# Experts of a slot mixture on one Trainium2 core: dense inner values, up products transposed in four row tiles, two batches, the first one's outputs inside the loop

## The chip, the core and the metric

One core of a Trainium2 chip runs the kernel. Its engines work side by side, each through its own list of instructions: TensorE (PE) multiplies matrices into PSUM, VectorE (DVE), ScalarE (ACT) and GpSimd (POOL) do elementwise work and reductions, SyncE (SP) issues the transfers. Semaphores order them. The metric is the device time of one execution in microseconds; less is better.

## The reference

A small vision tower: 32 images of 36 patches, 1152 tokens of width 192, in float32. The change lies in the last part, the mixture of 8 experts with 4 slots each:

```python
Xn = l2_normalize(X, axis=-1)
sp = l2_normalize(slot_params, axis=1) * scale
logits = jnp.einsum('bmd,dnp->bmnp', Xn, sp)
D = jax.nn.softmax(logits, axis=1)
C = jax.nn.softmax(logits.reshape(b, m, n * p), axis=2).reshape(b, m, n, p)
X_tilde = jnp.einsum('bmd,bmnp->bnpd', Xn, D)
H = gelu(jnp.einsum('bnpd,ndh->bnph', X_tilde, W_down) + b_down[None, :, None, :])
Y_tilde = jnp.einsum('bnph,nhd->bnpd', H, W_up) + b_up[None, :, None, :]
Y = jnp.einsum('bnpd,bmnp->bmd', Y_tilde, C)
```

Ahead of it stand a patch embedding with two layer norms and a channel attention with a residual and a norm; behind it come another residual and the last norm. Each expert has 24 inner values.

## The kernel before

The tokens are worked on in 11 groups of three images (108 tokens; the last has two images, 72). Every step of the computation is a function of a group `g`, and the order on each engine is written out by hand: a loop over `s` calls the functions with staggered groups (`at(slot_in, s - 6)` works on group s - 6), in 17 steps on TensorE and ACT and 16 on DVE and POOL. Nothing is reordered by a scheduler; an engine that waits holds everything behind it.

For a group, the end of the loop is this chain. `turn_xn` (PE, L507) transposes the unit tokens xn, `take_xn` (ACT) copies them, `logits` (PE, L519) multiplies with the slots. `mask_logits` gives lm on DVE, from which come two softmaxes: mC, eC (over slots) and, by way of `turn_l` (L526), mD, eD (over tokens). DVE inverts the sums (rC, rD) and scales eD, `turn_dc` (L535, L536) transposes both, DVE takes dm and ACT takes cT, `slot_in` (L542) forms the slots' inputs, and `take_slots` copies them to xt (ACT, L1018). A table load on ACT stands wherever exponentials and gelus alternate.

The experts are worked in three batches of groups, `HB = ((0, 4), (4, 8), (8, NG))`. `hidden(b)` (L554) multiplies xt with the down weights: expert n lands in column tile n % 4, on 24 of its 32 partitions, and e = n // 4 is the half of the free axis. `gelu(b)` (L1026) writes `hb[128, 2, B, 8, 4]` one expert at a time into an array that was cleared before, so that each column (slot of expert n) is zero except on its own expert's 24 partitions. By this the up product of a group is two full products with all of hb as weights: `slot_out(g)` (L565), out of 96 slots by 192. The bias is added on DVE (`slot_bias`, yt, L855), `combine(g)` (L578) multiplies with cT, and DVE's `last_residual` (z, L862), `last_stats` (L870) and `last_moments` (L875), POOL's `ln4_root` (L1139, L1142), DVE's `last_shift` (L880) and ACT's `last_norm` (o, L1035) finish the group; SP sends it out.

hidden(0) and hidden(1) stand in TensorE's steps 13 and 14, gelu(0) in ACT's step 15, behind the last exponentials. All outputs come after the loop, eleven rounds of slot_out and combine. POOL clears wu and hb at the start.

## Time and profile before

| what | us |
|---|---|
| median of 3 runs | 141.26 (140.8 to 141.6) |
| profiled execution | 140.0 |
| its span, first to last instruction | 138.0 |
| PE busy in the span | 115.0 |
| DVE busy | 88.9 |
| ACT busy | 69.0 |
| POOL busy | 67.0 |

The busy times are sums over stages with different limits; PE's is not a measure of how near it is to its peak, since its matmuls are pipelined. The stages must be read one at a time: weights and inputs to about 33 us, the loop to about 117, the outputs from there.

### The profile page before, as it was taken

What the parts mean: (1) busy time and instruction counts of PE and PEld (TensorE: products, weight loads), DVE (VectorE), ACT (ScalarE), POOL (GpSimd) and SP (SyncE); (2) the same over time, 40 slices, a digit from 0 to 9 for tenths busy, and PEclk for the clock granted to TensorE, in tenths of its full rate; (3) what the DMA queues carried; (4) which work ended last, traced back from release to release, by engine and by line L of the source; (5) the groups of instructions that cost most, each with busy time, mean ns of one, the idle gap of its engine ahead of it and who ended that gap; (6) DMA issues with size and microseconds to landing.
All of it is one profiled execution on the core that took longest, in us unless ns stands there. A gap on an engine that the chain in (4) does not pass through costs nothing.

```text
span 138.0 us, 4819 instructions
## 1 busy us (share of the span) xinstructions
PE 115.0 (83%) x1779; PEld 93.6 (68%) x1779; DVE 88.9 (64%) x380; ACT 69.0 (50%) x234; POOL 67.0 (49%) x158
## 2 busy tenths in 40 slices
PE   0297799999699999999999999997986860999920
PEld 0297799888377868578787796866964630788700
DVE  0211999999643687985857558586987440159980
ACT  3000004242862848648675686846644468763553
POOL 8500277767847428837265382743664000007871
PEclk9999999999999999999999999999999555599995
DMA  1999899988000000000000000000000000000232
GB/s 14 337 293 278 269 305 320 314 319 214 5 7 0 5 0 7 5 0 7 0 5 5 0 5 0 10 5 0 5 0 7 0 0 0 5 0 24 72 89 71
DMA packets 7677, 10.34 MB, mean 75 GB/s; under 512 B 2056, under 2 KB 5032, under 8 KB 7656
## 3 DMA queue, kind: packets, MB, share of 16 engines
q1 hardware_dynamic: 7656, 10.06, 24.2%
q8 instruction: 14, 0.23, 0.7%
q14 instruction: 7, 0.06, 0.1%
HBM read 9.17 MB, written 0.88 MB: 73 GB/s over the span
## 4 chain that ended last, share of the span: by engine, by line
PE 47%; DVE 22%; issue 12%; POOL 10%; ACT 4%; DMA 3%; SPq 1%; POOLq 1%; DVEq 0%; ACTq 0%
DVE st L649 8%; PE ps L565 7%; PE ps L436 6%; PE ps L476 5%; PE ps L496 3%; PE ps L542 3%; PE ps L399 3%; DMA wt<-in_w_tok 3%; PE ps L489 3%; PE ps L519 3%; DVE y L663 3%; PE ps L578 3%; DVE st L671 2%; PE ps L507 2%; PE ps L407 2%
## 5 line engine op out<-in xcount | busy, mean ns | idle before, releaser
L417 PE MATMUL ps<-wc,xT 128*108 128x192 f32 (+1 forms) x132 | 23.0, 327 | 1.5 <-DVE wc L637 1.5
L940 ACT ACTIVATE hT<-ps,b,g 96x108 f32<-96x108 f32 (+1 forms) x22 | 8.4, 430 | 27.9 <-PE ps L426 27.9
L417 PEld LDWEIGHTS ps<-wc,xT 128*108 128x108 f32 (+1 forms) x132 | 20.7, 170 | 2.0 <-DVE wc L637 1.8
L436 PE MATMUL ps<-wqk,hT 96*108 96x384 f32 (+1 forms) x44 | 16.2, 490 | 0.7 <-ACT qp L962 0.7
L1125 POOL TENSOR_SCALAR pw<-mv 108x1 f32<-108x1 f32 (+1 forms) x11 | 3.7, 337 | 21.3 <-DVE mv L780 21.3
L476 PE MATMUL ps<-hT,wv 96*128 96x108 f32 (+1 forms) x88 | 12.5, 284 | 0.0
L1139 POOL TENSOR_SCALAR var<-mv 108x1 f32<-108x1 f32 (+1 forms) x11 | 2.4, 223 | 18.9 <-DVE mv L875 18.4
L950 ACT ACTIVATE sq<-ps 108x384 f32<-108x384 f32 (+1 forms) x11 | 5.4, 490 | 12.4 <-PE ps L436 12.4
L476 PEld LDWEIGHTS ps<-hT,wv 96*128 96x128 f32 x88 | 10.7, 191 | 0.7
L649 DVE BATCH_NORM_STATS2 st<-xs 108x6 f32<-108x384 f32 (+1 forms) x22 | 10.9, 540 | 0.2 <-issue 0.2
L960 ACT ACTIVATE km<-ps,imgsel 108x192 f32<-108x192 f32 (+1 forms) x32 | 11.0, 418 | 0.0
L565 PE MATMUL ps<-wu,hb 128*96 128x192 f32 (+1 forms) x44 | 10.6, 375 | 0.0
L542 PE MATMUL ps<-dm,xn 108*96 108x96 f32 (+1 forms) x44 | 6.7, 284 | 3.9 <-ACT cT L1013 3.9
L1082 POOL TENSOR_SCALAR var<-mv 108x1 f32<-108x1 f32 (+1 forms) x11 | 2.4, 222 | 15.3 <-DVE mv L655 15.3
L436 PEld LDWEIGHTS ps<-wqk,hT 96*108 96x108 f32 (+1 forms) x44 | 6.8, 171 | 4.1 <-issue 1.6
L1035 ACT ACTIVATE o<-z,sh,rstd 108x192 f32<-108x192 f32 (+1 forms) x11 | 6.0, 546 | 6.4 <-DVE sh L880 6.4
L399 PE MATMUL ps<-wt,b 128*128 128x192 f32 x12 | 4.2, 538 | 6.0 <-DMA wt<-in_w_tok 6.0
L496 PE MATMUL ps<-wp,yT 128*108 128x192 f32 (+1 forms) x44 | 9.1, 330 | 0.0
L542 PEld LDWEIGHTS ps<-dm,xn 108*96 108x96 f32 (+1 forms) x44 | 5.6, 194 | 4.3 <-issue 3.6
L834 DVE RECIPROCAL rC<-sC 108x1 f32<-108x1 f32 (+1 forms) x11 | 1.8, 162 | 10.3 <-ACT eD L1006 10.3
L565 PEld LDWEIGHTS ps<-wu,hb 128*96 128x96 f32 (+1 forms) x44 | 7.3, 184 | 1.5 <-issue 0.7
L399 PEld LDWEIGHTS ps<-wt,b 128*128 128x128 f32 x12 | 3.7, 333 | 5.9 <-issue 5.9
(106 smaller groups left out, 304.6 us busy)
## 6 DMA issues: line engine op xcount, KB each, us to landing
xT<-in_x_t SPq DMA_DIRECT2D x10, 324.0 KB, 7.0
xs<-in_x SPq DMA_DIRECT2D x10, 324.0 KB
out<-o SPq DMA_DIRECT2D x10, 81.0 KB
wt<-in_w_tok SPq DMA_DIRECT2D x1, 576.0 KB, 4.2
wqk<-in_w_qk SPq DMA_DIRECT2D x1, 288.0 KB, 8.7
xT<-in_x_t SPq DMA_DIRECT2D x1, 216.0 KB, 7.5
xs<-in_x SPq DMA_DIRECT2D x1, 216.0 KB
wv<-in_w_v SPq DMA_DIRECT2D x1, 192.0 KB, 9.0
```

Source lines behind the costliest of these rows:

```text
L399: mm = pe.matmul(bwp(), b1[:, kc:kc + 1].broadcast_to([128, 128]), wt[:, kc, :], start=kc == 0, stop=kc == KC - 1)
L417: mm = pe.matmul(tokp(g), xT[:, o + kc * n:o + (kc + 1) * n], wc[:, kc, :], start=kc == 0, stop=kc == KC - 1)
L436: mm = pe.matmul(qkp(g), hT[:, f, t0:t0 + tokens(g)], wqk[:, f, :, :, :].rearrange("p j h d -> p (j h d)"), start=f == 0, stop=f == 1)
L476: mm = pe.matmul(vp(g)[:, m, :], wv[:, f, 4 * m:4 * m + 4, :].rearrange("p h d -> p (h d)"), hT[:, f, t0:t0 + tokens(g)], start=f == 0, st ...
L496: mm = pe.matmul(prp(g), yT[:, g % NY, m, 0:images(g), :].rearrange("p i n -> p (i n)"), wp[:, m, :], start=m == 0, stop=m == 1)
L542: mm = pe.matmul(xtlp(g)[:, f, :], xn[0:tokens(g), g, f * F:(f + 1) * F], dm[0:tokens(g), g % NX, 0:images(g) * SL], start=True, stop=True)
L565: mm = pe.matmul(ytp(g), hb[:, e, i0:i0 + ni, :, :].rearrange("p i n q -> p (i n q)"), wu[:, e, :], start=e == 0, stop=e == 1)
L649: ins = dve.bn_stats(st1[0:n, g % 2, h, :], xs[0:n, g % NB, h * (PD // 2):(h + 1) * (PD // 2)])
L940: ins = act.activation(hT[:, f, t0:t0 + tokens(g)], htp(g)[:, f, :], ACT.Identity, bias=b2[:, f:f + 1], scale=g2[:, f:f + 1])
L950: act.activation(sq[0:n, g % 2, :, :, 0:DH].rearrange("p j h d -> p (j h) d"), p, ACT.Square).then_inc(sq_ready, 1)
L960: act.activation(km[0:n, g % NK, i, :], qkp(g)[:, D:2 * D], ACT.Copy, scale=imgsel[0:n, i:i + 1])
L1035: act.activation(o4[0:n, g % NQ, :], z2[0:n, g % NQ, :], ACT.Identity, bias=sh4[0:n, g:g + 1], scale=rstd4[0:n, g:g + 1]).then_inc(o4_read ...
```

## The change

The experts are laid out in another way, and the work is cut in two batches, `HB = ((0, 6), (6, NG))`.

- **Down product and gelu.** Expert n = 2j + e goes to column tile j and half e. The down weights are padded to 32 columns, so all 128 partitions are written; hb has one column for an image's slot, [128, 2, 72], with no zeros between experts, and a batch needs two gelus (128 partitions, 72 or 56 columns) in place of eight. The up weights are padded to 32 rows in the input and come in one transfer. The clears of wu and hb and SP's wait for them are gone.
- **Up product.** `widen(b)` computes it transposed: 16 products with weights of 32 rows (the expert's inner values) by 96 columns (half of the width), each on one of four row tiles, over the batch's 72 or 56 columns, into four banks of PSUM. DVE (`take_upper`) and ACT (`take_lower`) each copy half of it to `uT`, 576 or 448 elements on 96 partitions. `turn_u(g)` transposes a group's 96 columns back, two halves, into the place of slot_out's result.
- **Order.** hidden(0) and gelu(0) stand in step 12, widen(0) and its copies in step 13. turn_u and the bias of groups 0 to 5 come in pairs in steps 14, 15 and 16, combine and the rest one step later. hidden(1), widen(1) and groups 6 to 10 come after the loop. In that last part DVE runs z, statistics and moments of the same group in a row.

```diff
-HB = ((0, 4), (4, 8), (8, NG))
+HB = ((0, 6), (6, NG))
+NBI = 18
+HS = 12
+WIDE = {14: (0, 1), 15: (2, 3), 16: (4, 5)}
...
-        hb = sb("hb", [128, 2, B, NE, NP])
+        hb = sb("hb", [128, 2, NBI * NP])
+        uT = sb("uT", [F, NE * 2 * NBI * NP])
...
-            sp.wait_ge(cleared, 6)
-            for j in range(4):
-                sp.dma_start(wu[32 * j:32 * j + HID, :, :], w_up[j]).then_inc(experts_in, 16)
+            sp.dma_start(wu[:, :, :].rearrange("p e d -> p (e d)"), w_up).then_inc(experts_in, 16)
...
                 for n in range(NE):
-                    j = n % 4
+                    j = n // 2
                     for f in range(2):
-                        mm = pe.matmul(hp(b, i1 - i0)[32 * j:32 * j + HID, n // 4, :, :], wd[:, f, n, :],
+                        mm = pe.matmul(hp(b, i1 - i0)[32 * j:32 * j + 32, n % 2, :], wd[:, f, n, :],
                                        xt[:, f, i0:i1, n, :], start=f == 0, stop=f == 1,
                                        tile_position=(0, 32 * j))
...
+            def widen(b):
+                i0, i1 = batch(b)
+                pe.wait_ge(hb_ready, b + 1)
...
+                if b >= 1:
+                    pe.wait_ge(yt_ready, HB[b][0])
+                    pe.wait_ge(z2_ready, HB[b][0])
+                for e in range(2):
+                    for f in range(2):
+                        for j in range(4):
+                            r = slice(32 * j, 32 * j + 32)
+                            mm = pe.matmul(utp(i1 - i0)[:, j, f, :, e, :], wu[r, e, f * F:(f + 1) * F],
+                                           hb[r, e, 0:(i1 - i0) * NP], start=True, stop=True,
+                                           tile_position=(32 * j, 0))
+                mm.then_inc(utp_ready, 1)
+
+            def turn_u(g):
+                b = sum(g >= e for _, e in HB[:-1])
+                i0 = (g - HB[b][0]) * GI
+                pe.wait_ge(uT_lower, b + 1)
+                pe.wait_ge(uT_upper, b + 1)
                 if g >= 2:
                     pe.wait_ge(yt_ready, g - 1)
...
+                for f in range(2):
+                    u = widened(b)[:, f, i0:i0 + images(g), :, :]
+                    mm = pe.transpose(ytp(g)[:, f * F:(f + 1) * F],
+                                      u.rearrange("p i j s -> p (i j s)"), ident[0:F, 0:F])
...
+            def take_upper(b):
+                i0, i1 = batch(b)
+                dve.wait_ge(utp_ready, b + 1)
+                if b >= 1:
+                    dve.wait_ge(ytp_ready, HB[b][0])
+                dve.tensor_copy(widened(b)[:, :, :, 2:4, :].rearrange("p f i j s -> p j (f i) s"),
+                                utp(i1 - i0)[:, 2:4, :, :, :, :].rearrange("p j f i e q -> p j (f i) (e q)")).then_inc(uT_upper, 1)
...
-                for n in range(NE):
-                    r = slice(32 * (n % 4), 32 * (n % 4) + HID)
-                    ins = act.activation(hb[r, n // 4, i0:i1, n, :], hp(b, i1 - i0)[r, n // 4, :, :],
-                                         ACT.Gelu, bias=bd[r, n // 4:n // 4 + 1])
+                if b >= 1:
+                    act.wait_ge(utp_ready, b)
+                for e in range(2):
+                    ins = act.activation(hb[:, e, 0:(i1 - i0) * NP], hp(b, i1 - i0)[:, e, :],
+                                         ACT.Gelu, bias=bd[:, e:e + 1])
...
-            pool.memset(hb[:, :, :, :, :], 0.0).then_inc(cleared, 1)
```

Three places show the new order.

On ACT, steps 12 and 13 of the loop, before (cT and xt are the copies for a group's slots, eC and eD the exponentials):

```order
L1018 ACTIVATE xt<-ps 96x2x96
L1013 ACTIVATE cT<-ps 96x108
L1000 ACTIVATE eC,sC<-lm,mC 108x96
L1006 ACTIVATE eD,sD<-ps,mD 96x108
L993 ACTIVATE xnT<-ps 96x216
```

The same place in the changed kernel:

```order
L1082 ACTIVATE xt<-ps 96x2x96
L1091 ACT_TABLE_LOAD
L1091 ACTIVATE hb<-ps,bd 128x72 x2
L1077 ACTIVATE cT<-ps 96x108
L1064 ACT_TABLE_LOAD
L1064 ACTIVATE eC,sC<-lm,mC 108x96
L1070 ACTIVATE eD,sD<-ps,mD 96x108
L1057 ACTIVATE xnT<-ps 96x216
```

The first batch's gelus moved here from step 15, with a table load ahead of them, which carries the wait for hidden(0), and one behind cT, for the exponentials. A third load stands ahead of gelu(1), without the wait for its product.

On TensorE, before, the last two steps and the first rounds behind the loop (L519 is logits, L535 and L536 turn_dc, L526 turn_l, L542 slot_in, L565 slot_out, L554 hidden, L578 combine):

```order
L519 MATMUL ps<-sp,xnT 72x64 x2
L535 MATMUL ps<-ident,eD 108x96
L536 MATMUL ps<-ident,eC 96x108
L526 MATMUL ps<-ident,lm 64x72
L542 MATMUL ps<-dm,xn 96x96 x2
L535 MATMUL ps<-ident,eD 72x64
L536 MATMUL ps<-ident,eC 64x72
L542 MATMUL ps<-dm,xn 96x64 x2
L565 MATMUL ps<-wu,hb 96x192 x4
L554 MATMUL ps<-xt,wd 24x32 x16
L565 MATMUL ps<-wu,hb 96x192 x2
L578 MATMUL ps<-yt,cT 108x192
```

The same place in the changed kernel (L541 logits, L557 and L558 turn_dc, L548 turn_l, L564 slot_in, L611 turn_u, L620 combine):

```order
L611 MATMUL ps<-ident,uT 96x96 x4
L541 MATMUL ps<-sp,xnT 72x64 x2
L557 MATMUL ps<-ident,eD 108x96
L558 MATMUL ps<-ident,eC 96x108
L548 MATMUL ps<-ident,lm 64x72
L564 MATMUL ps<-dm,xn 96x96 x2
L620 MATMUL ps<-yt,cT 108x192 x2
L611 MATMUL ps<-ident,uT 96x96 x4
L557 MATMUL ps<-ident,eD 72x64
L558 MATMUL ps<-ident,eC 64x72
L564 MATMUL ps<-dm,xn 96x64 x2
L620 MATMUL ps<-yt,cT 108x192 x2
```

Two transposes and two combines of the first batch now stand between one step's slot_in and the next step's turn_dc.

On DVE, one round behind the loop, before (yt is the bias, st and mv statistics and moments, sh the shift):

```order
L855 TENSOR_TENSOR yt<-ps,bu 96x192
L870 BN_STATS st<-z 108x6
L880 SCALAR_TENSOR_TENSOR sh<-mv,rstd 108x1
L862 SCALAR_TENSOR_TENSOR z<-ps,rC,z 108x192
L875 BN_AGGR mv<-st 108x2
```

And a round of groups 6 to 10 in the changed kernel:

```order
L906 TENSOR_TENSOR yt<-ps,bu 96x192
L913 SCALAR_TENSOR_TENSOR z<-ps,rC,z 108x192
L921 BN_STATS st<-z 108x6
L926 BN_AGGR mv<-st 108x2
L931 SCALAR_TENSOR_TENSOR sh<-mv,rstd 108x1
```

The statistics now read the z written by the instruction right in front of them, and the moments those statistics; before, another group's work stood between.

## Rows read from the trace of the kernel before

**Rows 1.** The page: its head and its clock row in 40 slices.
```profile
span 138.0 us, 4819 instructions
...
PEclk9999999999999999999999999999999555599995
```

**Rows 2.** Table by stretches: span's us, length, busy us and counts by engine, granted clock.
```profile
100.00:104.00 4.00, 2.99 (x52) 2.19 (x49) 3.40 (x19) 1.51 (x7) 2.30 (x5) 1.00 0.00 0
...
108.00:112.00 4.00, 3.51 (x48) 2.73 (x48) 1.24 (x7) 1.76 (x10) 0.00 (x0) 0.50 0.00 0
...
121.00:126.00 5.00, 5.00 (x35) 4.52 (x30) 3.56 (x15) 2.74 (x9) 1.62 (x4) 0.98 0.00 0
```

**Rows 3.** The chain that ended last, 104 to 122: start us, us, what.
```profile
109.76 0.67 PE ps L519 x4
...
112.88 1.28 ACT L1026
...
114.17 0.29 ACT hb L1026
...
116.62 0.23 ACT cT L1013
...
117.87 2.61 PE ps L565 x8
```

**Rows 4.** Timeline of DVE: start us, us, line, operation, count, idle before.
```profile
105.55 0.16 DVE L834 RECIPROCAL rC<-sC 108x1 f32<-108x1 f32 x1 [0.51 <-ACT eD L1006]
...
107.27 0.25 DVE L819 TENSOR_REDUCE mC<-lm 108x1 f32<-108x96 f32 x1
...
122.34 0.42 DVE L862 SCALAR_TENSOR_TENSOR z<-ps,rC,z 108x192 f32<-108x192 f32 x1 [1.47 <-PE ps L578]
...
131.96 0.41 DVE L862 SCALAR_TENSOR_TENSOR z<-ps,rC,z 108x192 f32<-108x192 f32 x1
...
132.40 0.36 DVE L870 BATCH_NORM_STATS2 st<-z 108x6 f32<-108x192 f32 x1
...
132.74 0.41 DVE L862 SCALAR_TENSOR_TENSOR z<-ps,rC,z 72x192 f32<-72x192 f32 x1
...
133.18 0.36 DVE L870 BATCH_NORM_STATS2 st<-z 72x6 f32<-72x192 f32 x1
...
133.57 0.18 DVE L875 BATCH_NORM_AGGREGATE mv<-st 72x2 f32<-72x6 f32 x1
```

**Rows 5.** Timeline of TensorE's matmuls, 100 to 123.
```profile
100.60 0.47 PE L489 MATMUL ps<-vT,pc 32*32 32x37 f32 x32
...
105.15 0.50 PE L542 MATMUL ps<-dm,xn 108*96 108x96 f32 x4
105.58 0.57 PE L554 MATMUL ps<-xt,wd 96*24 96x48 f32 x32
...
121.81 0.49 PE L578 MATMUL ps<-yt,cT 96*108 96x192 f32 x2
122.14 0.81 PE L565 MATMUL ps<-wu,hb 128*96 128x192 f32 x4
```

**Rows 6.** Timeline of ACT, 102 to 119.
```profile
102.02 0.33 ACT L1018 ACTIVATE xt<-ps 96x192 f32<-96x192 f32 x1
...
104.67 0.37 ACT L1000 ACTIVATE eC<-lm,mC 108x96 f32<-108x96 f32 x1
...
118.21 2.43 ACT L1026 ACTIVATE hb<-ps,bd 24x48 f32<-24x48 f32 x8
```

**Rows 7.** Timeline of DVE near the start: one subtraction that reads PSUM.
```profile
13.17 1.35 DVE L637 TENSOR_TENSOR wc<-wg,ps 128x1152 f32<-128x1152 f32 x1 [5.76 <-PE ps L407]
```

**Rows 8.** Timeline of POOL: first work behind the memsets, and the last.
```profile
16.26 0.22 POOL L1082 TENSOR_SCALAR var<-mv 108x1 f32<-108x1 f32 x1 [10.80 <-DVE mv L655]
...
134.54 0.57 POOL L1142 TENSOR_TENSOR rstd<-var,mhalf 72x1 f32<-72x1 f32 x1
```

More of the change, by code:

```diff
@@ L54, in at, with wide, batch @@
         stage(g)
+def wide(s):
+    return WIDE.get(s, ())
+def batch(b):
+    return HB[b][0] * GI, min(B, HB[b][1] * GI)
 def images(g):
@@ L557, in hidden @@
                 mm.then_inc(hp_ready, 1)
-            def slot_out(g):
-                i0, ni = g * GI, images(g)
-                pe.wait_ge(hb_ready, 1 + sum(g >= e for _, e in HB[:-1]))
+            def widen(b):
+                i0, i1 = batch(b)
+                pe.wait_ge(hb_ready, b + 1)
+                if b == 0:
+                    pe.wait_ge(v_ready, NG)
+                    pe.wait_ge(lnn_ready, NG)
+                    pe.wait_ge(e2_scaled, NG)
+                if b >= 1:
[14 more added lines that the diff above has]
+                pe.wait_ge(uT_upper, b + 1)
                 if g >= 2:
                     pe.wait_ge(yt_ready, g - 1)
-                for e in range(2):
-                    mm = pe.matmul(ytp(g), hb[:, e, i0:i0 + ni, :, :].rearrange("p i n q -> p (i n q)"),
-                                   wu[:, e, :], start=e == 0, stop=e == 1)
+                for f in range(2):
+                    u = widened(b)[:, f, i0:i0 + images(g), :, :]
+                    mm = pe.transpose(ytp(g)[:, f * F:(f + 1) * F],
+                                      u.rearrange("p i j s -> p (i j s)"), ident[0:F, 0:F])
                 mm.then_inc(ytp_ready, 1)
@@ L607, in _ @@
                 at(norms, s)
-                if s == NG + 2:
-                    pe.wait_ge(experts_in, 16 * (3 + 4))
-                    pe.wait_ge(qk_ready, NG)
+                if s == HS:
+                    pe.wait_ge(experts_in, 16 * (3 + 1))
                     hidden(0)
-                if s == NG + 3:
-                    pe.wait_ge(v_ready, NG)
-                    hidden(1)
-            pe.wait_ge(lnn_ready, NG)
-            pe.wait_ge(e2_scaled, NG)
-            slot_out(0)
-            slot_out(1)
-            hidden(2)
-            for g in range(2, NG):
-                slot_out(g)
-                combine(g - 2)
-            combine(NG - 2)
+                if s == HS + 1:
+                    widen(0)
+                for g in wide(s - 1):
+                    combine(g)
+                for g in wide(s):
+                    turn_u(g)
+            hidden(1)
+            combine(4)
+            combine(5)
+            widen(1)
+            turn_u(6)
+            for g in range(7, NG):
+                turn_u(g)
+                combine(g - 1)
             combine(NG - 1)
@@ L894, in _ @@
             slot_sums()
-            for s in range(16):
+            for s in range(HS + 6):
                 if s == 4:
@@ L923, in _ @@
                 at(residual_moments, s - 2)
-            slot_bias(0)
-            slot_bias(1)
-            for g in range(2, NG + 4):
-                at(last_residual, g - 2)
-                at(last_moments, g - 3)
+                if s == HS + 1:
+                    take_upper(0)
+                for g in wide(s - 1):
+                    last_residual(g)
+                for g in wide(s):
+                    slot_bias(g)
+                for g in wide(s - 1):
+                    last_stats(g)
+                    last_moments(g)
+                for g in wide(s - 2):
+                    last_shift(g)
+            take_upper(1)
+            for g in wide(HS + 4):
+                last_shift(g)
+            slot_bias(6)
+            for g in range(7, NG + 3):
                 at(slot_bias, g)
-                at(last_stats, g - 2)
-                at(last_shift, g - 4)
+                at(last_residual, g - 1, 6)
+                at(last_stats, g - 1, 6)
+                at(last_moments, g - 1, 6)
+                at(last_shift, g - 2, 6)
         @block.scalar
```

59 lines of the change are left out of this document (38 added, 21 removed).

## The prediction

> **What bounds the kernel now.** I read the page first. The profiled execution spans 138.0 us and was timed at 140.0; the clock row holds full speed for 31 slices of 3.45 us, to 107 us, then shows four slices of half speed [rows 1]. Nothing that the diff touches runs before about 101 us, apart from loads and memsets, so I read from there on. The table by stretches says that TensorE was busy 3.0 of 4 us in 100 to 104 at full clock (2.4 GHz), that the clock had fallen to 0.50 (1.2 GHz) in 108 to 112, and that it was back at 0.98 in 121 to 126 [rows 2].
>
> The chain of waits then gives the price of the experts as they are. After the last exponentials ACT loads the gelu table for 1.28 us at 112.88 and runs eight gelus of some 0.3 us; only then, at 116.62, does it copy the last group's cT, on which TensorE's last slot product waits [rows 3]. Eight records of the up product at half clock follow (2.61 us) [rows 3]. The first final residual (z, L862) starts at 122.34 and the eleventh at 132.74: 1.04 us a group for ten rounds. From there to the end of the span are 5.26 us [rows 4]. So the bound has three pieces: a stretch of 9.5 us between 112.9 and 122.3 in which no output is made, eleven rounds at 1.04, and the drain. In a round TensorE and DVE are equally full: a combine takes 0.33 from its start to the next up product's start [rows 5], the up product the rest of the 1.04.
>
> **The change: gelus and tables.** 24 gelus on 24 partitions become four on 128. Eight take 2.43 us [rows 6], or 0.30 each, mostly independent of width, so I price a gelu of 72 or 56 columns at 0.31 and the four at 1.25 in place of 7.2. Against that, the first batch now stands in step 12 of the loop, with exponentials behind it: one table load becomes three. ACT finishes the copy xt of group 6 at 102.35 [rows 6]. hidden(0) begins on TensorE at that copy's start, 101.9. The load of the gelu table waits for its product, since the wait stands on the load, so nothing of it hides. Thus: product ready 102.7, load to 104.0, two gelus to 104.6, cT of group 7 to 104.8, load of the exponentials' table to 106.1. Before, eC of group 8 started at 104.67 [rows 6]. It comes **1.4 us later**. The third load does not wait for hidden(1), and the product it precedes is late by more than 1.28: I cost it at nothing. If that cover were gone it would cost 1.28.
>
> The trace shows one load: it begins 0.02 us behind the work before it and the first gelu starts 1.29 after it, at 114.17, with no drain around it [rows 3]. The Trainium skill says otherwise (ScalarE: Activation LUTs, section on what ACT_TABLE_LOAD costs): 1283 ns and a drain of about 1380 ns at every switch of set. By that page the two loads inside the loop would cost 2.8 us more; it is a rival below.
>
> **The loop's last steps.** DVE waits for eD of group 8 before rC (105.55), and from there to mC of group 9 (107.27) is 1.72 us [rows 4]. Now eC is at 106.1 and rC, 0.88 behind it as before, at 107.0. Of the 1.72, some 0.4 was a wait for POOL that will be over. take_upper(0) is new before mC: 576 elements from PSUM. The nearest row is 1152 elements in 1.35 us [rows 7], so about 0.75; runs of eight elements might double it. mC of group 9 then starts at 107.0 + 1.3 + 0.75 = 109.0, **1.8 later**. The lower half of the copy runs on ACT meanwhile; xt's 192 elements take 0.33 [rows 6], so 0.65 to 1.0, in a gap in which ACT waits for DVE.
>
> TensorE from 107 on is at half clock, as it was, because it idles at least as much. Prices at full clock: four records with 96 moving columns 0.43 (105.15 to 105.58) [rows 5], so a turn_u (two records) 0.22 and a combine 0.33; at half clock twice that. In order: the turn of xn 10 at 109.4, slot_in(8) to 110.6, turn_u(0) and (1) to 111.45, logits(10) (0.67 [rows 3]) to 112.1, turn_dc(9) to 112.45; DVE takes dm 9 and adds the biases of groups 0 and 1 by 113.5; slot_in(9) to 114.15, combine(0) and (1) to 115.45, turn_u(2) and (3) to 116.3, turn_dc(10) to 116.65, dm 10 to 117.05. z of group 0 stands behind dm 10 on DVE, so the **first residual comes at 117.05** instead of 122.34: 5.3 us early although the softmax part itself is late.
>
> **The middle.** DVE then works in pairs: two z, two biases, twice statistics and moments. Statistics start 0.44 behind the z they read, and moments 0.39 behind their statistics [rows 4]; moments wait for statistics here with nothing between, so a pair costs 0.7 + 0.5 + 0.95 + 0.25 = 2.4, and the last of the three pairs is in work when batch 1 begins. TensorE beside it has two combines, two turn_u (0.66 + 0.44 at full clock, twice that at half) and once hidden(1), 0.4 to 0.75. It is dense from 113.3 on, and before, the clock was back about 4 us after it became dense at 117 [rows 2, 3]; I take it back by the time of widen(1). Widen(1) waits for z of group 5 (ended by 122.4: 117.05, two pairs of 2.4 and one z), takes 0.9 and 0.2 to land (123.5); the copies take 0.6, turn_u(6) 0.4, its bias 0.3, combine(6) 0.5, each with its landing: z of group 6 starts at about 125.3.
>
> **The price of widening.** No row shows 32-row tiles with 96 output columns. Between two bounds: 32 records in one batch, each as long as one of slot_in's (96 columns of weights, 0.11), in turn 3.5 us; four at a time 0.9. The nearest row is the attention's mix, in 32 by 32 tiles on the diagonal: 32 records in 0.47 us [rows 5]. At 37 columns one alone would need 0.032 (0.33 for two of 192 columns), so 1.0 in turn; its tiles overlap. I take 0.9, which for batch 0 lies under the wait for the late xnT of group 9. hidden has 72 columns, 0.062 a record, 2.0 in turn and 0.5 overlapped; before, 32 of 48 columns took 0.57 [rows 5] where 1.3 were due in turn. Runs on one tile grow from four records to eight; I keep the overlap. A page's rule speaks against the row tiles: the Trainium skill (TensorE: Matmul & The Clock Gate, LDWEIGHTS) times a weight load by its columns alone, 32 rows as 128, so by it (an estimate) 80 ns a record, and widening wins nothing unless loads of different row tiles run at once.
>
> **The last five groups.** z, statistics and moments of a group now stand directly behind one another on DVE: 0.25 (bias) + 0.44 + 0.39 + 0.2 = 1.28 a round instead of 1.04 [rows 4]. That order costs 0.24 a round, about 1.0 in all, and makes DVE the bound; TensorE's 0.55 a round hides beneath it. z of group 10 comes at 125.3 + 4 x 1.28 = 130.4, less 0.2 since its round has no bias: 130.2, against 132.74. Then the drain: before, POOL lagged (its last root ended at 135.11) behind groups whose z came 0.78 apart at the end [rows 4, 8]; at 1.28 it keeps up (its root takes 0.57), and the drain is 4.6 instead of 5.26.
>
> **Sum.** 130.2 + 4.6 = 134.8 for the span, **3.2 less**. At the start, memsets of wu and hb go from POOL, whose next work waited 10.8 us for DVE anyway [rows 8], and four small loads become one: nothing. The median is 141.26, 1.26 above the profiled execution's own 140.0; less 3.2 is **138.0 us**.
>
> **Rivals.** (1) *Row tiles do not overlap* (slower). Widen(0) ends at 105.6 + 3.7 = 109.3 instead of being covered until 107.3, +2.0; widen(1) +2.6 at full clock. 138.0 + 4.6 = 142.6, and 145 at half clock. It decides from about 3.3 us of the sum, that is from two thirds of the records in turn. For it: the rule on weights, and that four tiles now write the same output partitions in four banks. Against: the mix. Chance 0.13. (2) *Runs of eight on one column tile do not overlap*: hidden(0) +1.4 on the way to the gelus, hidden(1) +1.1 to 2.3: about 141, the same as before. Chance 0.08. (3) *A drain at each table switch*: 138.0 + 2.8 = 140.8, the same. For it only the page; against it the load in the trace [rows 3]. Chance 0.05. (4) *The early outputs don't come early*: the copies with runs of eight cost double (+1.4) and the clock stays at half through the middle (+1.5, widening, turns and combines of the hand-over at twice their price): 140.9. Chance 0.06. (5) *The clock never falls*, since TensorE has more to do in 102 to 115: the half-clock steps above shrink by some 2.5 us: 135.5; this is inside my forecast's range.
>
> **How the numbers follow.** Forecast 0.68, 135 to 140. A measurement here can tell about 0.5% (0.7 us) from no change. Faster takes the forecast and some of (4): 0.71. Same takes (2), (3) and parts of the rest: 0.14. Slower is (1) and its mixtures with (2): 0.15. The range 135.0 to 141.0 leaves out (1) and little else.
>
> **What would show each step.** The second table load in front of an eC at about 104.8; eC 8 at 106.1; z of group 0 near 117; the widening's 32 records in under 1.2 us; rounds of 1.28 at the end; last z near 130.2 and the drain under 4.8. I am wrong if the widening takes over 2.5 us, if the gelus start later than 104.5, or if TensorE, not DVE, is what the last rounds wait for.

## The result and the profile after

| what | before | changed |
|---|---|---|
| median of 20 runs each, us | 141.52 | 142.19 |
| ratio to before, 95% interval | | 1.0148 (1.0088 to 1.0208) |
| profiled execution, us | 140.0 | 141.36 |
| its span | 138.0 | 139.5 |
| mean granted clock of TensorE in it | 0.939 | 0.887 |

The changed kernel is slower by 1.5%, where 138.0 us and a gain of 2.3% were forecast. Ratios here and below are not the quotients of the medians, since they leave out executions that were disturbed (for the kernel before, in the last batch of experiments, 24 of 29).

The page of the changed kernel, its head and its clock row in 40 slices of 3.49 us (the counterpart of [rows 1]):

```profile
span 139.5 us, 4826 instructions
...
PEclk9999999999999999999999999999999555555555
```

Before, the row had four slices of half speed and full speed again behind them. Now there are nine, and no return. The table by stretches says the same more finely (columns as in [rows 2]: start and end, length, busy us and count of PE, its weight loads, DVE, ACT, POOL, then the granted clock):

```profile
104.00:108.00 4.00, 2.87 (x48) 2.23 (x46) 1.66 (x8) 3.89 (x10) 1.67 (x4) 0.99 0.00 0
108.00:112.00 4.00, 2.73 (x13) 2.13 (x14) 3.00 (x15) 2.29 (x9) 0.00 (x0) 0.50 0.01 2
112.00:116.00 4.00, 3.51 (x20) 2.99 (x19) 1.94 (x10) 1.65 (x7) 0.00 (x0) 0.50 0.00 0
116.00:120.00 4.00, 3.28 (x16) 2.58 (x15) 2.09 (x8) 0.76 (x3) 0.17 (x1) 0.50 0.00 0
120.00:124.00 4.00, 4.00 (x41) 3.46 (x40) 2.57 (x11) 1.53 (x3) 2.86 (x8) 0.50 0.01 4
124.00:128.00 4.00, 2.62 (x37) 1.94 (x36) 2.60 (x11) 0.81 (x2) 1.66 (x5) 0.50 0.00 0
128.00:132.00 4.00, 3.80 (x15) 2.73 (x16) 2.64 (x9) 2.36 (x6) 0.79 (x2) 0.50 0.44 124
```

The clock falls at about the same time as before, at 107.9 instead of 107.5. From 112 to 132 TensorE is busy for 2.6 to 4.0 us of four, and it still works at 1.2 GHz to its last product.

The chain of waits of the changed kernel shows what that touches (L578 is hidden, L1091 the gelus, L1064 the exponentials, L620 combine, L597 widen):

```profile
102.20 1.47 PE ps L578 x32
103.74 1.28 ACT L1091
105.03 0.53 ACT hb L1091 x2
105.68 0.23 issue
105.91 1.28 ACT L1064
...
121.41 2.03 PE ps L578 x32
123.43 1.56 PE ps L620 x4
...
125.58 1.58 PE ps L597 x32
```

And DVE's timeline gives the landmarks of the prediction (L898 take_upper, L913 the final residual z), beside [rows 4]:

```profile
109.87 0.74 DVE L898 COPY uT<-ps 96x576 f32<-96x576 f32 x1
...
118.00 0.73 DVE L913 SCALAR_TENSOR_TENSOR z<-ps,rC,z 108x192 f32<-108x192 f32 x2
...
125.02 0.42 DVE L913 SCALAR_TENSOR_TENSOR z<-ps,rC,z 108x192 f32<-108x192 f32 x1 [0.22 <-PE ps L620]
...
129.89 0.42 DVE L913 SCALAR_TENSOR_TENSOR z<-ps,rC,z 108x192 f32<-108x192 f32 x1 [0.75 <-PE ps L620]
...
134.66 0.41 DVE L913 SCALAR_TENSOR_TENSOR z<-ps,rC,z 72x192 f32<-72x192 f32 x1
```

The first output does come early, at 118.0 instead of 122.34. But from there to group 6's residual pass 11.9 us; the kernel before started all eleven of its residuals in 10.4.

### The profile page after: what moved, and what is told of

Its sections match the earlier page's. It is cut to its first block, busy times and chain, and to the rows that moved or that the text cites. A ratio compares the mean times of both kernels' runs of the same rounds, so it can differ in the third digit from the quotient of the medians.

```text
span 139.5 us, 4826 instructions
## 1 busy us (share of the span) xinstructions
PE 117.2 (84%) x1789; PEld 94.4 (68%) x1789; DVE 91.9 (66%) x382; ACT 66.3 (48%) x218; POOL 64.6 (46%) x156
## 4 chain that ended last, share of the span: by engine, by line
PE 46%; DVE 15%; DMA 15%; issue 10%; POOL 6%; ACT 5%; SPq 1%; POOLq 1%; DVEq 0%; ACTq 0%
DMA xs<-in_x 12%; PE ps L458 6%; PE ps L498 5%; PE ps L620 4%; DVE st L692 4%; PE ps L564 3%; PE ps L518 3%; PE ps L541 3%; DMA wt<-in_w_tok 3%; PE ps L511 3%; PE ps L421 3%; PE ps L578 3%; PE ps L529 3%; PE ps L487 2%; DVE z L913 2%
## 5 line engine op out<-in xcount | busy, mean ns | idle before, releaser
L620 PE MATMUL ps<-yt,cT 96*108 96x192 f32 (+1 forms) x22 | 9.4, 558 | 0.5 <-DVE yt L906 0.3
L421 PE MATMUL ps<-wt,b 128*128 128x192 f32 x12 | 3.6, 479 | 6.1 <-DMA wt<-in_w_tok 6.1
L564 PE MATMUL ps<-dm,xn 108*96 108x96 f32 (+1 forms) x44 | 6.7, 283 | 1.2 <-ACT cT L1077 1.2
L1109 ACT ACTIVATE o<-z,sh,rstd 108x192 f32<-108x192 f32 (+1 forms) x11 | 5.5, 541 | 4.3 <-DVE sh L931 4.3
L541 PE MATMUL ps<-sp,xnT 96*108 96x96 f32 (+1 forms) x44 | 6.9, 286 | 0.7 <-ACT xnT L1057 0.7
L758 DVE TENSOR_TENSOR sc<-rn,rqt 128x144 f32<-128x144 f32 (+1 forms) x11 | 4.0, 363 | 5.2 <-POOL rqt L1192 5.2
```

What stands on the lines that cost most here:

```text
L421: mm = pe.matmul(bwp(), b1[:, kc:kc + 1].broadcast_to([128, 128]), wt[:, kc, :], start=kc == 0, stop=kc == KC - 1)
L541: mm = pe.matmul(lgp(g), xnT[:, g % NX, f, 0:tokens(g)], sp3[:, f, 0:images(g), :, :].rearrange("p i n q -> p (i n q)"), start=f == 0, sto ...
L564: mm = pe.matmul(xtlp(g)[:, f, :], xn[0:tokens(g), g, f * F:(f + 1) * F], dm[0:tokens(g), g % NX, 0:images(g) * SL], start=True, stop=True)
L620: pe.matmul(yop(g), cT[0:images(g) * SL, g, 0:tokens(g)], yt[0:images(g) * SL, g % NQ, :], start=True, stop=True).then_inc(yop_ready, 1)
L1109: act.activation(o4[0:n, g % NQ, :], z2[0:n, g % NQ, :], ACT.Identity, bias=sh4[0:n, g:g + 1], scale=rstd4[0:n, g:g + 1]).then_inc(o4_read ...
```

## How the experiments are compared

From one profiled execution to the next the start of hidden(0) stands anywhere between 102.1 and 106.6 us, in kernels whose code ahead of it is the same (b2, where hidden(0) stands later, is left aside). That would drown what is to be measured. So beside the timed ratio to the kernel before I give the **stretch**: from the start of hidden(0), or for the kernel before the same place, behind slot_in of group 6, to the end of the span. Stretches are of one execution each; ratios, of 6 to 12 runs, are the check on them. Each ratio is to the kernel before on the same chip, and the batches a, b and c ran on three different chips. "First z" is the distance from the start of hidden(0) to the residual of group 0. "Clock falls" is the distance from the start of the stretch to the fall of the granted clock; "no" means that it is full until TensorE's last product.

| kernel | stretch | clock falls | first z | z 6 to z 10 | ratio to before | mean clock, all runs |
|---|---|---|---|---|---|---|
| before | 36.1 | 5.6 | | 4.11 | 1 | 0.919 to 0.963 |
| changed | 37.4 | 5.8 | 15.9 | 4.77 | 1.0148 | 0.876 to 0.902 |
| a1 hidden's order | 34.9 | 7.2 | 14.5 | 4.77 | 1.0014 (0.9966 to 1.0062) | 0.884 to 0.913 |
| a2 fillers | 31.0 | no | 12.95 | 4.66 | 0.9745 (0.967 to 0.9821) | 0.963 to 0.984 |
| a3 round order | 36.1 | 7.0 | 15.3 | 3.79 | 1.0123 (1.0048 to 1.0198) | 0.873 to 0.901 |
| a4 no gelu | 35.1 | 9.5 | 13.6 | 4.77 | none | 0.886 to 0.953 |
| b1 a1 + a2 | 30.1 | no | 12.2 | 4.67 | 0.9786 (0.9738 to 0.9833) | 0.977 to 0.983; 1.0 in one of 221.92 us |
| b2 all outputs late | 41.5 | 3.9 | | 4.77 | 1.0507 (1.042 to 1.0595) | 0.859 to 0.877 |
| b3 a1 + a2 + a3 | 29.5 | no | 12.15 | 3.55 | 0.9699 (0.9638 to 0.976) | 0.976 to 0.988 |
| b4 before + fillers | 33.2 | no | | 4.11 | 0.9919 (0.987 to 0.9968) | 0.978 to 0.989 |
| c1 early fillers only | 33.0 | 15.6 | 12.95 | 4.77 | 0.9958 (0.9897 to 1.0019) | 0.904 to 0.967 |
| c2 late fillers only | 30.9 | no | 12.9 | 4.67 | 0.9937 (0.9835 to 1.004) | 0.935 to 0.989 |
| c3 b3 + early table load | 29.4 | no | 12.16 | 3.55 | 0.9718 (0.9622 to 0.9814) | 0.978 to 0.992 |
| c4 a1 + a3 | 34.7 | 5.5 | 15.0 | 3.78 | 1.0031 (0.9973 to 1.0089) | 0.886 to 0.901 |

Two cautions go with this table. Set against the one profiled execution of the kernel before, the stretches come out 0.8 to 4.3 us better than the timed ratios do (a1: 1.2 us shorter, where the ratio says 0.2 us longer). So whether a kernel beats the one before is read from the ratio. And the moment of the fall differs between kernels that are alike or nearly so up to there, 5.5 to 7.2 us behind the start of hidden(0) in four of them, and what it brings along isn't the edit's: a3's first z is 0.6 us earlier than the changed kernel's, though its edit touches only the last rounds.

The expectations below often name the right branch and miss its size: a2 gave twice what was expected of it, while b1 (0.965 expected), b3 (0.95 to 0.96), b4 (0.98) and c4 (0.98 to 0.995) gave less against the kernel before. In c2 the expected fall of the clock isn't in the profile.

My theory after the result: the half clock (1.2 GHz, 0.50 in the rows) is what turns the gain into a loss, since the changed kernel stays in it for 31 us and the one before for 14. The rivals: the two passes of hidden cost too much, the table loads do, the order of the last rounds does, or the early outputs aren't worth their place.

## Experiments on the clock

**a2, idle products in TensorE's waits.** A filler multiplies the identity with itself, into a bank of PSUM whose content is no longer needed; nothing reads it. There are 26 in all.

```diff
+            def filler(bank, k):
+                for _ in range(k):
+                    pe.matmul(ps[:, bank, 0:128], ident[:, :], ident[:, :], start=True, stop=True)
...
+                if s == 13:
+                    pe.wait_ge(v_ready, NG)
+                    filler(1, 4)
+                if s == 14:
+                    filler(4, 4)
                 at(turn_xn, s - 4)
+                if s in (15, 16):
+                    filler(4, 2 if s == 15 else 3)
...
                     widen(0)
+                    pe.wait_ge(z_ready, NG)
+                    filler(4, 3)
...
             combine(5)
+            pe.wait_ge(hb_ready, 2)
+            filler(4, 3)
             widen(1)
+            filler(4, 3)
             turn_u(6)
             for g in range(7, NG):
                 turn_u(g)
+                filler(4, 1)
                 combine(g - 1)
```

> The changed kernel plus idle matmuls of the identity with itself (128 columns, never read) in TensorE's waits from step 13 on: 4, 3, 4, 2, 3, 3, 3 and one a round; everything else is the same, and all outputs are computed. If the clock, which stays at 0.5 from 108 us to the end, is what the middle and the tail lack: it comes back somewhere between 110 and 125, combines of 0.65 become 0.33, and the span falls by 1.5 to 3 us although the fillers delay some steps by 0.1 to 0.3. If the steps from 118 on are paced by DVE and not by TensorE: the clock may rise but the span moves by under 0.7. If the clock does not rise, the fillers only delay: 0 to 1.5 us longer.

Measured: the ratio is 0.9745, the stretch 31.0, 6.4 us shorter. The table by stretches of a2, where the changed kernel had 0.50:

```profile
108.00:112.00 4.00, 3.83 (x59) 3.45 (x58) 1.84 (x10) 3.89 (x11) 1.66 (x4) 1.00 0.00 0
112.00:116.00 4.00, 3.80 (x36) 3.13 (x35) 3.17 (x16) 2.34 (x10) 0.00 (x0) 1.00 0.01 2
116.00:120.00 4.00, 3.96 (x30) 3.24 (x30) 2.77 (x13) 1.46 (x8) 0.00 (x0) 1.00 0.02 4
```

and its timeline of TensorE at the hand-over to the second batch:

```profile
121.08 1.26 PE L578 MATMUL ps<-xt,wd 96*32 96x56 f32 x32
122.28 0.90 PE L620 MATMUL ps<-yt,cT 96*108 96x192 f32 x4
...
124.10 0.90 PE L597 MATMUL ps<-hb,wu 32*96 32x56 f32 x32 [0.23 <-DVE z L930]
```

Four records of combine take 0.90 instead of 1.6, widen 0.90 instead of 1.55. Work was added, and what stood there before became shorter by a factor of 1.7 to 1.8, where the clocks differ by 2. Beside the fillers only the waits for a semaphore ahead of some of them are new.

**b4, the same in the kernel before.** A comparison with a2 alone would be unfair, since the kernel before also has a stretch at half clock. It gets 21 fillers.

```diff
+                if s == 13:
+                    pe.wait_ge(v_ready, NG)
+                    filler(1, 3)
+                if s == 14:
+                    pe.wait_ge(z_ready, NG)
+                    filler(4, 4)
                 at(turn_xn, s - 4)
+                if s in (15, 16):
+                    filler(4, 4 if s == 15 else 10)
                 at(slot_in, s - 6)
```

> The kernel before with idle matmuls in its own waits from step 13 on (3, 4, 4 and 10), no other edit. Its clock is at half from 107 to 121 us. If the clock's fall is a loss of its own that fillers give back in either kernel: the steps between 107 and 121 (slot products of 0.9, the first eight up products of 2.6) halve and it gains 1.5 to 3 us, ratio about 0.98. If before waits in that stretch for ACT's gelus whatever TensorE's speed: under 1 us, since only the up products at 117.9 to 121 shorten.

Measured: 0.9919, and a stretch of 33.2, 2.9 us shorter. The first eight records of the up product, 2.61 us on the chain before [rows 3] (2.82 in the timeline), are in b4

```profile
116.94 1.49 PE L565 MATMUL ps<-wu,hb 128*96 128x192 f32 x8
```

Thus with fillers in both the change gains 33.2 - 31.0 = 2.2 us by the stretches, and 0.9919 to 0.9745, or 2.5 us, by the timed runs. That is the direction of the forecast and some three quarters of its 3.2 us, though the forecast was against the kernel before with its own half clock. By the stretches fillers give 6.4 us to the changed kernel and 2.9 to the one before. The difference, 3.5, is more than the gain of 2.2, and the 1.3 that are left are what the two stretches differ by. By the timed ratios the same sum is 5.7 and 1.1, a difference of 4.6 against a gain of 2.5, which leaves the 2.1 us by which the changed kernel is slower.

**c1 and c2, which fillers.** c1 keeps the first 11, of steps 13 and 14; c2 keeps the other 15.

Against a2, c1 has this in the loop, and none of the fillers behind it:

```diff
-                    filler(4, 2 if s == 15 else 3)
+                    filler(4, 0 if s == 15 else 0)
```

And c2 this, in steps 13 and 14:

```diff
-                    filler(1, 4)
+                    filler(1, 0)
...
-                    filler(4, 4)
+                    filler(4, 0)
...
-                    filler(4, 3)
+                    filler(4, 0)
```

> The changed kernel with the idle matmuls of steps 13 and 14 alone (4, 3 and 4), none later. It tells whether the loss is the fall of the clock at 108 us, or that it does not come back. If the fall is all: the clock stays full from 108 on, the span is as with all fillers (30.9 us from the start of hidden(0) to the end, against 37.4 with none). If TensorE's work from 112 on is too thin by itself to hold the clock: it falls later, between 112 and 125, and the result lies between, 33 to 36.

> The changed kernel with the idle matmuls of steps 15 and 16 and behind the loop alone (2, 3, 3, 3 and one a round), none before. The clock falls at 107 to 108 as in the changed kernel. If it comes back once TensorE is dense again, as it did in the kernel before at 121: between 115 and 122, and 32 to 35 us from hidden(0) to the end. If it stays at half: 37 to 38.5, the fillers only delay.

Measured, c1: 0.9958, stretch 33.0. The table by stretches of c1:

```profile
112.00:116.00 4.00, 3.48 (x31) 2.67 (x29) 3.20 (x15) 1.99 (x9) 0.00 (x0) 1.00 0.01 2
116.00:120.00 4.00, 3.08 (x22) 2.59 (x23) 2.74 (x14) 1.79 (x9) 0.00 (x0) 1.00 0.02 4
120.00:124.00 4.00, 3.87 (x42) 2.99 (x40) 3.16 (x15) 1.51 (x3) 3.11 (x8) 0.62 0.00 0
124.00:128.00 4.00, 2.62 (x37) 2.18 (x38) 2.73 (x12) 1.93 (x5) 1.55 (x4) 0.50 0.02 5
```

Behind the part with fillers the clock falls after all, at 121.0. That is 16 us behind the start of hidden(0), where in the changed kernel it was 6. So there is a second place at which the changed kernel can lose it, and early fillers don't cover it.

c2: 0.9937, with a stretch of 30.9, as a2. Its own table:

```profile
108.00:112.00 4.00, 2.51 (x46) 1.95 (x45) 2.09 (x13) 3.88 (x12) 1.66 (x4) 1.00 0.00 0
112.00:116.00 4.00, 2.89 (x26) 2.17 (x25) 3.20 (x15) 2.06 (x9) 0.00 (x0) 1.00 0.01 2
```

In this execution the clock didn't fall before TensorE's last product, with the same thin work by which it fell in the changed kernel's profile. (c2 keeps the semaphore waits of the early fillers, so these stand in it as well.) But over the runs of c2 the mean clock goes from 0.935 to 0.989, the profiled one being the highest, and the ratio is 0.019 above a2's, which was timed on another chip. In part of the runs the clock may fall early, as without fillers; no trace shows such a run. The mean clock can't settle it either, since it also counts a fall far ahead of this stretch, which was found in half of the profiles and lowers it by up to 0.025, and the fastest run of c2, 137.04 us, has 0.954. One profile is no proof that the clock stays up.

## Experiments on hidden

**a1, another order of the same 32 records.** Expert n lies in column tile n // 2, so in the order 0, 1, 2, ... eight records in a row go to one tile. Taking the even experts first makes it four, as before the change.

```diff
-                for n in range(NE):
+                for n in (0, 2, 4, 6, 1, 3, 5, 7):
```

> The changed kernel with one edit: hidden walks the experts in the order 0, 2, 4, 6, 1, 3, 5, 7, so that runs of four records, not eight, fall on one column tile. If runs of eight spoil the overlap of column tiles: the 32 records of hidden(0) take 0.7 to 0.8 us instead of 1.53, those of hidden(1) 0.9 to 1.1 at half clock instead of 2.10, the gelus of batch 0 start 0.8 earlier, the span is 1.5 to 2.0 us shorter (the second gain is on the way to z of group 4). If 32 columns in place of 24, or the wider moving side, cause the 1.53: both stay within 0.1 and the time does not move.

Measured: 1.0014, stretch 34.9, 2.5 us shorter. TensorE's timeline of the changed kernel has

```profile
102.13 1.53 PE L578 MATMUL ps<-xt,wd 96*32 96x72 f32 x32
...
121.34 2.10 PE L578 MATMUL ps<-xt,wd 96*32 96x56 f32 x32
```

and a1's, for the same records,

```profile
102.84 0.74 PE L578 MATMUL ps<-xt,wd 96*32 96x72 f32 x32
...
120.68 1.00 PE L578 MATMUL ps<-xt,wd 96*32 96x56 f32 x32
```

The first stands at full clock, the second at half. Runs of eight on one tile take twice as long as runs of four. The saved amounts, 0.79 and 1.10, make 1.9 us, and the timed ratios, 1.0148 to 1.0014, say 1.9 as well. The other 0.6 of the stretch isn't the order's: in this execution the clock fell 7.2 us behind the start of hidden(0), not 5.8, and the logits behind widen(0) were still at full clock. Changed, then a1:

```profile
108.29 1.03 PE L541 MATMUL ps<-sp,xnT 96*108 96x96 f32 x4 [0.67 <-ACT xnT L1057]
```

```profile
108.21 0.62 PE L541 MATMUL ps<-sp,xnT 96*108 96x96 f32 x4 [0.66 <-ACT xnT L1057]
```

This one line takes back the loss, and no more: TensorE is at half clock to the end.

**b1, both.** a2's fillers and a1's order.

> The changed kernel with both edits that helped: hidden in runs of four records, and the idle matmuls. Alone, measured from the start of hidden(0) to the end of the span, the order of hidden took 37.4 us to 34.9 and the fillers to 30.9. If they act on different things (record rate and clock): hidden(0) is 0.75 shorter at full clock and hidden(1), now at full clock, 0.5 shorter, so 30.0 or less, ratio to before about 0.965. If the shorter hidden only lets TensorE idle more and the clock falls again: 31 to 33, no better than the fillers alone.

Measured: 30.1 for the stretch, 0.85 less than a2. Of this 0.8 is there by the first z, from hidden(0). The second pass takes 0.64 instead of 1.26, but from the first z to that of group 6 it is 8.5 us in both: combine now waits for yt (0.30 us) and widen(1) for a z (0.52 us), so at full clock the second pass was covered. The order is worth less than half of its 1.9. The timed ratio, 0.9786, doesn't separate b1 from a2, whose interval overlaps it.

## Experiments on the last rounds

**a3, DVE's last rounds in the order of before.**

```diff
-            for g in range(7, NG + 3):
+            slot_bias(7)
+            for g in range(8, NG + 4):
+                at(last_residual, g - 2, 6)
+                at(last_moments, g - 3, 6)
                 at(slot_bias, g)
-                at(last_residual, g - 1, 6)
-                at(last_stats, g - 1, 6)
-                at(last_moments, g - 1, 6)
-                at(last_shift, g - 2, 6)
+                at(last_stats, g - 2, 6)
+                at(last_shift, g - 4, 6)
```

> The changed kernel with the last part of DVE (groups 6 to 10) in the order of the kernel before: z, moments of the group ahead, bias, statistics, shift of the one before. The prediction priced the new order at 0.24 us a round, 1.28 for 1.04. If that holds, the rounds, now 1.2, shrink to 1.04 and the end is 0.5 to 0.8 us earlier. If TensorE at half clock (combine and turn_u, 0.97 a round, and their latencies in a chain with the bias) is as long as DVE's round: under 0.3, or none, since z of a group then waits for its combine.

Measured: 1.0123, which the interval doesn't separate from the changed kernel. a3's timeline of DVE:

```profile
133.09 0.42 DVE L913 SCALAR_TENSOR_TENSOR z<-ps,rC,z 108x192 f32<-108x192 f32 x1 [0.75 <-PE ps L620]
...
136.88 0.41 DVE L913 SCALAR_TENSOR_TENSOR z<-ps,rC,z 72x192 f32<-72x192 f32 x1
...
139.22 0.16 DVE L931 SCALAR_TENSOR_TENSOR sh<-mv,rstd 72x1 f32<-72x1 f32 x1 [0.68 <-POOL rstd L1217]
```

Four rounds take 3.79 instead of 4.77 (0.95 instead of 1.19 each), but the drain grows from 4.8 to 5.15: the last sh waits for POOL's root, which comes 0.84 after the one ahead of it. A third of the microsecond is given back. That leaves 0.7 us of the 1.3 by which the stretch is shorter; the other 0.6 was there at the first z, by the later fall of the clock.

**c4, this order and a1's, without fillers.**

```diff
-                for n in range(NE):
+                for n in (0, 2, 4, 6, 1, 3, 5, 7):
...
-            for g in range(7, NG + 3):
+            for g in range(8, NG + 4):
```

> The order of hidden and DVE's last rounds in the old order, without fillers. Alone the first gave 37.4 to 34.9 us from hidden(0) to the end and the second 36.1. If both stand side by side at half clock: 34.0 or less, against 36.0 for the same stretch of the kernel before, ratio to before 0.98 to 0.995. If the clock at half makes TensorE the bound of the last rounds: no better than the first alone.

Measured: 1.0031, the same as before within its interval, at half clock to the end (0.886 to 0.901). The stretch is 34.7. The two edits do add: 37.4 less a1's 1.9 and a3's 0.7 is 34.8, and a1's own 34.9 had the later fall in it. Still, by the timed runs both cheap orders together don't make the change pay; the clock has to be kept.

## Experiments on the tables

**a4, Identity in place of Gelu.** It leaves out the gelu and with it all three table loads of the last part; the activations have the same size.

```diff
-                                         ACT.Gelu, bias=bd[:, e:e + 1])
+                                         ACT.Identity, bias=bd[:, e:e + 1])
```

> The changed kernel with Identity in place of Gelu in both batches, so that the function is left out and with it all three loads of ACT's tables; the four instructions stay. If the two loads inside the loop lie wholly on the path: eC of group 8 starts 2.5 us earlier and z of group 0 at least 1.8 earlier, the span 1.8 to 2.6 shorter. If there were a drain at a switch beside the load's 1.28, more: up to 5. If the loop's last steps are bound by TensorE instead (late turn and slot products at half clock), the gain dies out before z of group 0: under 1.0.

Measured: the stretch is 35.1, 2.3 us less, and the first z is 2.3 earlier. ACT's timeline of a4:

```profile
105.86 0.53 ACT L1091 ACTIVATE hb<-ps,bd 128x72 f32<-128x72 f32 x2 [1.19 <-PE ps L578]
107.74 0.26 ACT L1077 ACTIVATE cT<-ps 96x108 f32<-96x108 f32 x1 [1.35 <-DVE dm L891]
107.91 0.38 ACT L1064 ACTIVATE eC<-lm,mC 108x96 f32<-108x96 f32 x1
```

Two loads of 1.28 are gone, but between the gelus and cT there is now a wait of 1.35 for DVE: eC comes 3.7 us after the start of hidden(0) instead of 5.1. So the two loads together delay it by 1.4, not by 2.6, since cT's input isn't there sooner. The rest of the 2.3 comes behind eC: in this execution the clock fell 9.5 us behind the start of hidden(0), not 5.8, and the next logits were still at full clock (0.62 for four records, against 1.03).

**c3, b3 with the gelu table loaded ahead of the wait for hidden(0).**

```diff
+                if b == 0:
+                    act.preload_act_table_set("gelu_and_others")
                 act.wait_ge(hp_ready, b + 1)
```

> All three edits (order of hidden, fillers, DVE's last rounds) and the load of the gelu table issued ahead of the wait for hidden(0)'s product. There the load began 0.4 us after the copy before it had ended. If the load's place is on the path: eC of group 8 starts 0.4 earlier, measured from hidden(0), and the end is 0.3 to 0.4 earlier, too little for the times, to be read in the trace alone. If POOL's work or TensorE's turns take the slack: the end moves by under 0.1.

Measured: 0.9718 against b3's 0.9699, the same; the stretches are 29.4 and 29.5. c3's timeline of ACT:

```profile
105.41 1.28 ACT L1106 ACT_TABLE_LOAD   x1
106.70 0.53 ACT L1111 ACTIVATE hb<-ps,bd 128x72 f32<-128x72 f32 x2
107.68 0.26 ACT L1095 ACTIVATE cT<-ps 96x108 f32<-96x108 f32 x1 [0.45 <-DVE dm L908]
107.96 1.28 ACT L1082 ACT_TABLE_LOAD   x1
```

In b3 the load waited 0.44 for hidden(0); here it doesn't, and cT waits 0.45 for dm instead. A wait moved by 0.4 us, and what stood behind it came at the same time.

## Experiments on the placing, and the kernel that beats both

**b2, the new layout with all outputs behind the loop.**

```diff
-HS = 12
-WIDE = {14: (0, 1), 15: (2, 3), 16: (4, 5)}
+HS = 15
+WIDE = {17: (0, 1), 18: (2, 3), 19: (4, 5)}
...
-            for s in range(17):
+            for s in range(20):
```

> The changed kernel's layout, but the first batch behind the last exponentials: hidden(0) and gelu(0) in step 15, widening in 16, all outputs after the loop (their pairs in steps 17 to 19). It undoes the placement alone: one table load, and no turns or combines between the last softmax steps. If the early placement pays (the prediction's reading): z of group 0 comes at 120 or later instead of 118 and the end is 1 to 3 us later than the changed kernel's. If the two loads and TensorE's extra work in steps 13 to 16 eat the gain: the end is within 0.7 of it or earlier.

Measured: 1.0507, and a stretch of 41.5, 4.1 us longer than the changed kernel's. The early place of the first batch pays, even with its two extra table loads. That is shown with both at half clock; b2 with fillers was not run. b2 is at half clock from 108.7 on, 1.9 us sooner in its stretch than the changed kernel:

```profile
114.47 2.63 PE L578 MATMUL ps<-xt,wd 96*32 96x72 f32 x32
...
120.06 1.57 PE L597 MATMUL ps<-hb,wu 32*96 32x72 f32 x32
```

Each of these stands on the chain alone, where the changed kernel had its hidden(0) and widen(0) at full clock (1.53 and 0.91). The new chain of hidden, load, gelus, widening, copies and turns is longer than the old one and needs something to lie under.

**b3, a1's order, a2's fillers and a3's rounds together.** Its edit is the sum of the three diffs.

> Both edits and the last part of DVE in the order of the kernel before, which by itself brought z of group 6 to group 10 from 4.8 us to 3.8. If the three add: 29 us from hidden(0) to the end, ratio to before 0.95 to 0.96. If at full clock another engine (POOL with 0.85 a group) sets the end: no better than without it.

Measured: median 134.53 against 139.95 for the kernel before on the same chip, ratio 0.9699 (0.9638 to 0.976). **It beats both.** The page of b3, with the shares of the chain by engine:

```profile
PEclk9999999999977999999999999999999999999996
...
PE 40%; DVE 17%; DMA 15%; issue 11%; POOL 10%; ACT 4%; SPq 1%; POOLq 1%; DVEq 0%; ACTq 0%
```

Its rounds take 0.89 and POOL's two steps a group 0.85, so now POOL holds the end: its share of the chain is 10%, against 6% in the changed kernel.

## Why the prediction was wrong, step by step

The prediction put the span's end at 134.8; it came at 139.5. By its own landmarks:

| piece | predicted | measured | at full clock (a2) |
|---|---|---|---|
| start of hidden(0) | 101.9 | 102.13 | |
| hidden(0) to first z | 15.15 | 15.9 | 12.95 |
| first z to z of group 6 | 8.25 | 11.9 | 8.5 |
| z of group 6 to group 10 | 4.9 | 4.8 | 4.7 |
| last z to the end | 4.6 | 4.8 | 4.8 |

- **The step that failed** is "I take it back by the time of widen(1)". The clock stayed at 0.50 to the end. 3.6 of the 4.7 us are in the one piece that was to end at full clock, and a2, which has that clock, does it in 8.5 where 8.25 was forecast. Of the 3.6, 2.1 come by the end of group 5's z (at 125.4, forecast 122.4), where combine stood behind hidden(1) at half clock and DVE waited for it, and 1.5 behind it, in widen(1), the turns and combine(6). The inference was: before, the clock was back about 4 us after TensorE became dense, so it will be here. One return in one trace was taken for a rule. It was rival 4 that named this case, but priced it at 1.5 us and 0.06, because it counted only widening, turns and combines "of the hand-over" and not hidden(1), nor the waits between them, each of which ends behind a product at half speed. The Trainium skill (TensorE: Matmul & The Clock Gate, the section on a second failure mode of the gate) describes a kernel in which frequent short idle moments of TensorE between groups of products make its clock swing between the two levels. The prediction didn't weigh it. This trace agrees with the fall: from 102 on the waits that the rows show are below 1 us, and a1, a3, a4 and c2 show that when the clock falls there, or whether, differs from run to run. In the last stretch of the changed kernel, and of its variants in which the clock fell, no profile shows it coming back, as it does in the kernel that the Trainium skill describes.
- **hidden was mis-sized.** "0.5 overlapped" was 1.53, and "0.4 to 0.75" was 2.10 at half clock and 1.26 at full. "Runs on one tile grow from four records to eight; I keep the overlap" was wrong: a1 shows that the overlap is lost by just that. This is rival 2, priced at 1.4 plus 1.1 to 2.3; a1 measured 0.79 plus 1.10 at half clock. It was given 0.08. Because the rivals were added one at a time, the case that both 2 and 4 hold, which is what happened, had no chance of its own.
- **Widening was right.** 32 records took 0.91 at full clock, where 0.9 was taken from [rows 5]: 

```profile
106.70 0.91 PE L597 MATMUL ps<-hb,wu 32*96 32x72 f32 x32
```

  Row tiles overlap, and rival 1 falls. By the rule of the Trainium skill on weight loads (TensorE: Matmul & The Clock Gate, LDWEIGHTS) in turn the 32 would take an estimated 2.6. Here the loads of different row tiles ran side by side: the trace gives the 32 of them 159 ns each, which is 5.1 us, and 0.77 us busy in all.
- **The tables were right.** Loads of 1.28 at 103.74 and 105.91, the first gelu 1.29 after its load, the third load hidden behind hidden(1), as the prediction had it; no drain shows before or behind them. The Trainium skill (ScalarE: Activation LUTs, what ACT_TABLE_LOAD costs) has such a drain at every switch, and this trace doesn't agree; rival 3 falls, in all four kernels whose ACT timelines were read (before, changed, b3, c3). eC of group 8 came at 107.2 instead of 106.1, and hidden(0) explains 1.0 of that.
- **Gelus and copies were right.** Two gelus took 0.53 (0.62 forecast), the copies 0.74 and 0.64 (0.75, and 0.65 to 1.0).
- **Rounds and drain were right.** 1.19 a round for 1.28, and 4.8 for 4.6. a3 confirms that the order, not TensorE, sets the rounds, and that it was worth a microsecond there, of which POOL takes back a third.
- **The early outputs** were right in sign: b2 prices them at 4.1 us at half clock. That clears and small loads at the start cost nothing was not tried apart; hidden(0) began 0.2 us from where it was expected (half of that was the reading: the copy that it was put beside starts at 102.02 in [rows 6], not at 101.9).

What stays open is why the clock didn't come back in the changed kernel. Before, it was back at 121.2, 4.2 us after TensorE's work became dense, with eight 192-column records on all 128 rows and what follows. In the changed kernel TensorE is as dense between 118.5 and 125.0, in records on 96 rows, 192 columns wide or narrower, and the clock stays. That the kind of work matters is a guess that no run here separates from a mere difference in time.

The traces hold more on this than the last stretch. In seven of the fourteen profiles (a1, a2, a3, b1, b2, b3, b4) the clock also fell between 37 and 53 us, in code that no edit touches, and was full again 3 to 7 us later. In a1:

```profile
38.00:42.00 4.00, 4.00 (x15) 3.29 (x14) 1.13 (x3) 2.28 (x7) 2.57 (x4) 0.57 0.03 6
42.00:46.00 4.00, 4.00 (x76) 3.03 (x75) 2.35 (x7) 1.35 (x5) 1.63 (x4) 1.00 0.00 0
```

So the clock can come back in these kernels, and it can fall or not fall on the same instructions. This is a part of why executions differ, and why a mean clock over the whole span can't be read as the clock of the last stretch.

## What to carry to other kernels

Before cutting a dense block into smaller pieces that lie in the waits of a loop, ask what TensorE's clock will do, price the whole stretch behind the first fall at both levels, and give the worse one a chance that the trace can't rule out. Cheap idle products in the waits test it in one run, in the kernel before as well, and the comparison of the two with fillers is the worth of the change itself. Before a shorter stretch is put down to an edit, see whether the clock fell at the same place. With column tiles, let the program go on to another tile after four records rather than eight (fewer than four wasn't tried), and when rounds get faster ask which engine (here POOL) becomes the next bound.

## What was not expected of the hardware

- The same 32 fp32 records of 72 columns, on four column tiles, took 1.53 us in runs of eight on a tile and 0.74 in runs of four; of 56 columns at half clock, 2.10 and 1.00.
- The granted clock stayed at 0.50 for 31 us, with TensorE busy for 3.5 to 4.0 us of four in three of the stretches shown and 2.6 in the thinnest of them, and in all 20 runs of the changed kernel the mean clock was 0.876 to 0.902. In c2 it stayed at 1.00 with 2.5 us of four busy.
- In seven of fourteen profiles the clock also fell between 37 and 53 us and was full again 3 to 7 us later, on instructions that are the same in all kernels; in the other seven it stayed up there.
- 26 products that nobody reads, 52 of 1841 records, made the kernel 6.4 us shorter in its last stretch.
